# Transposes in two halves of 64 rows: probabilities and graph rows in a five-pass graph transformer

## The reference, cut to what matters

```python
x = _layernorm(x + _L0_gnn_ref(x, adj, adj, ...))   # 12-head attention, bias 2*adj, output product
x = _layernorm(x + _L1_gnn_ref(x, adj, ...))        # 12-head attention masked by adj > 0, no output product
x = _layernorm(x + _L2_gnn_ref(x, adj, ...))        # two graph layers, below
x = _layernorm(x + _L3_gnn_ref(x, adj, ...))        # 12-head attention, bias adj, output product

# one of the two graph layers
u = jnp.einsum('bid,bjd->bij', h, h) / temper
a = jax.nn.softmax(u, axis=-1)
delta = a * adjacency_matrix
attn = delta / (jnp.sum(delta, axis=-1, keepdims=True) + 1e-10)
hl, hs, hr = h @ wl.T + b_l, h @ ws.T + b_s, h @ wr.T + b_r
ctx = (attn * upper) @ hl + diag(attn)[..., None] * hs + (attn * lower) @ hr
h = jax.nn.relu(norm(ctx) * g + beta)
```

## Time and profile before

| | us |
|---|---|
| median of 3 executions | 2920.33 (2918.25 to 2920.56) |
| profiled execution, its own time | 2920.63 |
| its span, first to last instruction | 2918.9 |
| busy: PE matmul | 2676.6 (92%) |
| busy: PE weight load | 2351.3 (81%) |
| busy: DVE | 2204.6 (76%) |
| busy: ACT | 1441.8 (49%) |
| busy: POOL | 1906.2 (65%) |
| mean granted clock of PE | 0.963 |

### The profile page before, as it was taken

The page is one execution under the profiler, slowest core; times in us unless marked ns, Lnnn a source line. Parts: engine busy times, 40 slices in busy tenths (PEclk is TensorE's granted clock), DMA queues, the critical chain, the costliest instruction groups (busy, mean ns, idle before and its releaser), DMA issues. The chain is left out here.

```text
span 2918.9 us, 67000 instructions
## 1 busy us (share of the span) xinstructions
PE 2676.6 (92%) x22942; PEld 2351.3 (81%) x22942; DVE 2204.6 (76%) x3795; ACT 1441.8 (49%) x2968; POOL 1906.2 (65%) x2229
## 2 busy tenths in 40 slices
PE   7999999977999999599999888888887899999996
PEld 6888888866778778599999877777776688888885
DVE  4888888874777777577777667777777488888886
ACT  4555555535566666344444344444444455555553
POOL 2766766762666666577777567767776267766766
PEclk9999999988999999699999989999999999999998
DMA  3222222113222222312212132222221122222211
GB/s 108 70 67 68 66 66 68 55 42 96 78 76 81 81 76 63 99 53 68 64 55 67 56 102 71 69 68 71 69 68 48 57 70 67 68 66 68 66 58 39
DMA packets 179134, 200.54 MB, mean 69 GB/s; under 512 B 56516, under 2 KB 179016, under 8 KB 179016
## 3 DMA queue, kind: packets, MB, share of 16 engines
q1 hardware_dynamic: 179016, 198.99, 22.2%
HBM read 136.03 MB, written 62.91 MB: 68 GB/s over the span
## 5 line engine op out<-in xcount | busy, mean ns | idle before, releaser
L413 PE MATMUL l_ps_p<-l_xT,l_w 128*128 128x512 f32 x2592 | 677.5, 406 | 6.5 <-DVE l_xT L655 4.5
L1088 PE MATMUL l_ps_h<-l_w,l_hT 128*128 128x384 f32 x3456 | 678.9, 342 | 0.0
L1088 PEld LDWEIGHTS l_ps_h<-l_w,l_hT 128*128 128x128 f32 x3456 | 612.6, 191 | 2.6
L413 PEld LDWEIGHTS l_ps_p<-l_xT,l_w 128*128 128x128 f32 x2592 | 467.8, 189 | 110.7 <-issue 8.3
L342 POOL TENSOR_TENSOR l_pr<-l_sc,l_st 128x768 f32<-128x768 f32 x192 | 289.4, 1507 | 368.7 <-DVE l_st L693 341.1
L1178 ACT ACTIVATE l_hp<-l_hf 128x384 fp32r<-128x384 f32 x256 | 134.7, 526 | 474.5 <-DVE l_hf L1300 470.4
L312 POOL TENSOR_TENSOR v<-v,l_bvs 128x768 f32<-128x768 f32 x192 | 368.6, 1920 | 0.0
L999 POOL TENSOR_TENSOR l_hp<-l_hf,l_hp 128x384 fp32r<-128x384 f32 x256 | 272.0, 1062 | 134.4 <-ACT l_hp L1178 131.7
L407 PE MATMUL l_ps_p<-l_w,l_xT 128*128 128x384 f32 x1728 | 349.5, 347 | 7.6 <-ACT l_k L561 3.7
L574 ACT ACTIVATE v<-l_ps_p 64x192 f32<-64x192 f32 x768 | 250.5, 326 | 188.0 <-PE l_ps_p L407 179.1
L407 PEld LDWEIGHTS l_ps_p<-l_w,l_xT 128*128 128x128 f32 x1728 | 291.6, 188 | 27.3 <-issue 8.8
(11 more groups left out here) (129 smaller groups left out, 4761.1 us busy)
## 6 DMA issues: line engine op xcount, KB each, us to landing
rows<-l_yo SPq DMA_DIRECT2D x256, 192.0 KB, 1.9
l_xa<-rows SPq DMA_DIRECT2D x64, 768.0 KB, 5.0
l_xr<-rows SPq DMA_DIRECT2D x192, 192.0 KB, 2.4
l_xa<-in_x SPq DMA_DIRECT2D x16, 768.0 KB, 4.8
l_xr<-in_x SPq DMA_DIRECT2D x64, 192.0 KB, 2.4
out<-l_yo SPq DMA_DIRECT2D x64, 192.0 KB, 1.9
l_edge<-in_adj SPq DMA_DIRECT2D x80, 128.0 KB, 2.3
raw<-in_L_gnn_Wq SPq DMA_DIRECT2D x3, 576.0 KB, 5.8
```

The source lines that it names most:

```text
L413: last = nc.tensor.matmul(bank[:, :], W[m][:, l, t, o * P:(o + 1) * P], rows[:, r, t, :], start=c + t == 0, stop=c == 2 and t == KT - 1)
L1088: last = nc.tensor.matmul(ps_h[m][:, :D], hT[gpar][:, l, t, s * P:(s + 1) * P], W[m][:, r, t, :], start=c + t == 0, stop=m != SELF and c = ...
```

## The change

In `attention_pass`, `ps_t` becomes two tensors of one bank each, one for each graph of a unit. The six transposes of a unit become twelve: for each pair of heads one of the 64 rows of the first graph into the first bank, and one of the 64 rows of the second graph into the second. Both `pe_t` counts come at the last pair. ACT copies 384 elements from each bank. Before the transposes stands one wait for all older copies, and an instruction of its own that counts up a new semaphore, `pe_waited`, for which nobody waits.

In `digcn_pass`, the twelve transposes of a group become 24 in the same way, a bank for each graph. They are made in two steps: tiles 0 and 1 in unit 0 behind the left product, tile 2 in unit 1 behind the left product. ACT makes four copies for each step: 512 elements each in the first, 256 each in the second. The counts on `pe_x`, `act_x` and `act_f` are renumbered. This pass has a `pe_waited` too, counted up once ahead of each step. The transposes of rows in `attention_pass` (line 378), of attention (1073) and of weights stay whole.

```diff
+ROW_TILES = ((0, 1), (2,))
-        ps_t = a.ps("ps_t", [P, 2 * 512])
+        ps_t = [a.ps(f"ps_t{g}", [P, 512]) for g in range(GPU)]
...
@@ -440,13 +442,16 @@
                 if not inside(n, units):
                     return
                 pe.wait_ge(pool_p if wo else act_e, n + 1)
+                if counted(2 * n):
+                    pe.wait_ge(act_pT, 2 * n)
+                pe.sem_inc(pe_waited, 1)
                 for h in range(PAIRS):
-                    if h in (0, 4):
-                        if counted(2 * n - 1 + (h == 4)):
-                            pe.wait_ge(act_pT, 2 * n - 1 + (h == 4))
-                    last = nc.tensor.transpose(ps_t[:, h * P:(h + 1) * P], pr[b][:, 2 * h:2 * h + 2, :], ident[:, :])
-                    if h in (3, 5):
-                        last.then_inc(pe_t, 1)
+                    for g in range(GPU):
+                        q = slice(g * NODES, (g + 1) * NODES)
+                        last = nc.tensor.transpose(ps_t[g][:, h * NODES:(h + 1) * NODES], pr[b][q, 2 * h:2 * h + 2, :],
+                                                   ident[q, q])
+                        if h == PAIRS - 1:
+                            last.then_inc(pe_t, 1)
...
@@ -595,12 +600,12 @@
             def probs_T(n, b):
                 if not inside(n, units):
                     return
-                for half, (lo, hi) in enumerate(((0, 4), (4, 6))):
-                    act.wait_ge(pe_t, 2 * n + half + 1)
+                for g in range(GPU):
+                    act.wait_ge(pe_t, 2 * n + g + 1)
                     if counted(n - 1):
                         act.wait_ge(pe_o, n - 1)
-                    nc.scalar.activation(pT[b][:, lo:hi, :], ps_t[:, lo * P:hi * P].rearrange("p (h q) -> p h q", q=P),
-                                         ACT.Copy).then_inc(act_pT, 1)
+                    nc.scalar.activation(pT[b][:, :, g * NODES:(g + 1) * NODES],
+                                         ps_t[g][:, :D].rearrange("p (h q) -> p h q", q=NODES), ACT.Copy).then_inc(act_pT, 1)
...
-            sp.wait_ge(pe_x, KT)
+            sp.wait_ge(pe_x, 2)
...
-                        sp.wait_ge(pe_x, KT * (i + 2))
+                        sp.wait_ge(pe_x, 2 * (i + 2))
...
@@ -989,7 +995,7 @@
                 if not inside(g, groups):
                     return
                 for t in tiles:
-                    pool.wait_ge(act_x, KT * g + t + 1)
+                    pool.wait_ge(act_x, 4 * g + 2 + 2 * (t // 2))
...
-            def rows_T(g, gpar, tiles=range(KT)):
+            def rows_T(g, steps=range(2)):
                 if not inside(g, groups):
                     return
                 pe.wait_ge(s_xa, 16 * (g + 1))
-                for t in tiles:
-                    if counted(KT * g + t - 1):
-                        pe.wait_ge(act_x, KT * g + t - 1)
-                    for u in range(UNITS):
-                        last = nc.tensor.transpose(ps_x[(gpar + t) % 2][:, u * P:(u + 1) * P],
-                                                   xa[:, u, t * P:(t + 1) * P], ident[:, :])
+                for step in steps:
+                    if counted(4 * g + 2 * step):
+                        pe.wait_ge(act_x, 4 * g + 2 * step)
+                    pe.sem_inc(pe_waited, 1)
+                    for j, t in enumerate(ROW_TILES[step]):
+                        for u in range(UNITS):
+                            for b in range(GPU):
+                                q = slice(b * NODES, (b + 1) * NODES)
+                                c = (j * UNITS + u) * NODES
+                                last = nc.tensor.transpose(ps_x[b][:, c:c + NODES], xa[q, u, t * P:(t + 1) * P], ident[q, q])
                     last.then_inc(pe_x, 1)
 
...
-                pe.wait_ge(act_f, KT * (g + 1))
+                pe.wait_ge(act_f, 4 * (g + 1))
...
-                    pe.wait_ge(act_x, KT * (i + 1))
+                    pe.wait_ge(act_x, 4 * (i + 1))
...
-            rows_T(0, 0)
+            rows_T(0)
...
                     project(n, i, par, s, LEFT)
                     if s < 2:
-                        rows_T(i + 1, 1 - par, (2 * s,))
+                        rows_T(i + 1, (s,))
                     context(n - 1, ppar, ps)
                     project(n, i, par, s, RIGHT)
                     if s == 3:
                         attention_T(i + 1)
-                    if s == 0:
-                        rows_T(i + 1, 1 - par, (1,))
                     if s == 1:
                         products(i + 1, 1 - par)
                     project(n, i, par, s, SELF)
...
-            def rows_T(g, gpar, tiles=range(KT)):
+            def rows_T(g, gpar, steps=range(2)):
                 if not inside(g, groups):
                     return
-                for t in tiles:
-                    act.wait_ge(pe_x, KT * g + t + 1)
-                    bank = ps_x[(gpar + t) % 2]
-                    nc.scalar.activation(hF[gpar][:, t, :], bank[:, :], ACT.Copy).then_inc(act_f, 1)
-                    nc.scalar.activation(hT[gpar][:, 0, t, :], bank[:, :], ACT.Copy).then_inc(act_x, 1)
+                for step in steps:
+                    act.wait_ge(pe_x, 2 * g + step + 1)
+                    t, tiles = ROW_TILES[step][0], len(ROW_TILES[step])
+                    for b in range(GPU):
+                        bank = ps_x[b][:, :tiles * UNITS * NODES].rearrange("p (x q) -> p x q", q=NODES)
+                        for to, ready in ((hF[gpar][:, t:t + tiles, :], act_f), (hT[gpar][:, 0, t:t + tiles, :], act_x)):
+                            rows = to.rearrange("p t (u g q) -> p (t u) g q", g=GPU, q=NODES)[:, :, b, :]
+                            nc.scalar.activation(rows, bank, ACT.Copy).then_inc(ready, 1)
...
                     n, b = i * UNITS + s, s % 2
                     left_right(n, b, LEFT)
                     if s < 2:
-                        rows_T(i + 1, 1 - par, (2 * s,))
+                        rows_T(i + 1, 1 - par, (s,))
                     if s == 2:
                         attention(i + 1, 1 - par, 1)
                     normed(n - 2, pair * 4 + 2 * par + s // 2 - 1, b)
                     left_right(n, b, RIGHT)
-                    if s == 0:
-                        rows_T(i + 1, 1 - par, (1,))
                     standardise(n - 1, 1 - b)
```

More of the change, by code:

```diff
@@ L205, in attention_pass @@
         c_zero = a.sem("c_zero")
+        pe_waited = a.sem("pe_waited")
         pe_w, act_w, dve_w = a.sem("pe_w"), a.sem("act_w"), a.sem("dve_w")
```

## The result

The changed kernel takes 2930.08 us (median of 9 runs, 2927.82 to 2932.93). The kernel before, on the same chip, takes 2920.09. The ratio is 1.0033, 95% interval [1.0023, 1.0043]. The forecast was 2917.0 with a range from 2893 to 2940. The time lies in the range, but on the other side of no change. The profiled execution took 2932.93 us, with a span of 2931.0 us. It is the slowest of the nine, so the traces differ by 12.1 us where the medians differ by 10.0.

The account below looks back on a forecast made before the run. PE was taken to bound all but the second graph pass, where other engines set the pace. -6.3 + 1.7 + 1.2 = -3.4 us on 2920.63 us gave 2917, range 2893 to 2940.

Parts of the forecast that it names:

- In the second graph pass the 3.47 us cover it: Second graph pass: PE's 3.47 us wait for ACT's copies was said to hide the later rounding of the right product: 0.
- the third 256-element copy: Start of a graph pass: its end priced at 0.92 us, within 3.5 us from first copy to row products.
- Without cover it would be up to 16 x 0.62 = 10 us: Second graph pass: upper price of the later rounding if PE's wait did not hide it, up to 10 us.
- the rival of the counting instruction: PE's queue: the counting instruction after each wait holds the queue; +13 us, 2930 us, chance 0.18.
- Pace of the halves: Attention and graph passes: two half transposes run at once, 0.058 us a pair, against 0.109 for a whole one.
- That rival (0.109): Half transposes don't run side by side, 0.109 us a pair; +59 us, 2979 us, chance 0.08.
- Emptying: Weight block ahead of half transposes: the array empties at its end, 0.09 us.
- First load laid bare behind: Weight block behind half transposes: its first load is no longer hidden, 0.11 us.
- Three passes: The three attention passes, 48 groups at -0.132 us each: -6.3 us.
- the bound: Passes with an output product: most gain lost to transposes waiting for POOL's probabilities, 3 us; 0 was taken.
- First graph pass: First graph pass, PE always busy: seams outweigh the shorter stream by 0.11 us in 16 groups, +1.7 us.
- Starts: Starts of the two graph passes, where nothing hides the copies: 3.5 us instead of 2.94, together +1.2 us.

Follow-up runs that it names:

- e13: Changed kernel plus 24 matmuls of 256 columns, result never read, ahead of the products in the second graph pass: 2923.77 us.
- e5: Changed kernel with the counting instruction issued twice at each block of transposes instead of once: 2942.64 us.
- e7: Changed kernel, ACT's exact copies of both halves before the rounded ones, and unit 0's half 1 copies behind the rounding of the right product: 2919.54 us.
- e14: Kernel before, with POOL's three subtractions for the next group's rounded rows moved to the end of unit 2 in the second graph pass: 2901.71 us.
- e8: Changed kernel with ACT's exact copies of both halves ahead of both rounded ones in each graph-pass step: 2920.73 us.

## Why the prediction was wrong

**The failed step** is "In the second graph pass the 3.47 us cover it", with its 0. The 3.47 us are PE's wait for the copies. I had the rounding of the right product, and with it POOL, 0.62 us late, held that against PE's wait alone, and never asked whether the copies that end the wait come as early as before. They come 0.71 us later. One half was in my own numbers: I had the rounding end at 1425.9, so POOL begin later, but I followed only PE, who waits for that product, and not POOL's next instructions and what they do to DVE. The other half was in the same part too: at the start of the pass I priced the third 256-element copy, and in the steady groups I did not. The wait that I called a cover was the chain itself. (The two halves don't weigh the same: at full clock only DVE's is left, and the late copy costs through the clock alone, by e13.)

The clock is not in the prediction at all, though the earlier trace rows shows 0.95 there and 1.00 elsewhere; holding it up brought 10.8 us back (e13).

Two numbers of the prediction come near by chance. "Without cover it would be up to 16 x 0.62 = 10 us" is near the 11.9 measured, but it prices PE waiting for POOL's product. And the rival of the counting instruction stood at 2930, where the kernel landed, by +13 from that instruction; it took about 3, and the second graph pass the rest.

The other steps, by their own numbers:

- *Pace of the halves*, 0.058 us for a pair: a pair takes 0.062, the first 0.112, and a block and its seam take 0.52 us where I had 0.51. That rival (0.109) is out, and loads of 128 columns, two side by side, do not hold a pair at 0.107 us here.
- *Emptying*, 0.09: the weight block ahead of the transposes takes 0.095 more. Right.
- *First load laid bare behind*, 0.11: 0.02. Wrong in size. But the first load of a whole block, 0.06, was not on the path before either (0.63 from block to block, where I had 0.71), and so the difference holds: in the second pass units 0 and 1 gain 0.09 each (0.094), unit 2 loses 0.06 (0.056), unit 3 nothing (the wait took it, as said).
- *Three passes*, -6.3: they gave -0.2 a group in the second pass, against -0.13 (0.06 of it a shorter wait behind the values), and about -0.03 in the other two; with the first groups -1.5 us in all. There I handed back nothing to POOL, with 3 us as the bound. The counting instruction, which I took at 0 because the queue runs ahead, stands right behind that wait, where it can't run ahead: 0.10 a group. The rival was right in its mechanism on 64 of the 176 blocks I gave it, and wrong in the second pass, where a second one changed nothing (e5).
- *First graph pass*, +1.7: -0.3, or nothing. The two blocks take as long as the three did, and 0.095 is added ahead of each, but the seams around the third block, which is gone, give 0.19 back. I had today's three blocks at 1.31 us of stream, and from block to block they take 1.06.
- *Starts*, +1.2: +2.0. From the first copy to the products are 3.92 us in each pass, where I had 3.5.

Together these terms come to +0.2 where I had -3.4, so the change brings nothing even where the second graph pass loses nothing: e7, which has that pass back, took 2919.54 us, within the noise of before.

## What to carry to other kernels

An engine's idle time covers a delay only if what ends the idle time is not itself delayed: follow the changed order through the queue of each engine that it passes, to the copy that the wait names. In a stage where TensorE's granted clock is under 1.00, a late start is not worth its own length, but what the clock makes of it, and a shorter wait can pay more than it saves. VectorE operations with two inputs in SBUF and subtractions on GpSimd are worth moving apart; in this kernel that brought 18 us (e14).

## What the runs showed of the hardware that I had not expected

- The same 74 matmuls take 6.2, 7.5, 7.7 or 8.8 us, at granted clocks of 1.00, 0.80, 0.78 and 0.66, in a pattern that repeats every two or four groups. A start 0.27 us earlier changed the pattern, and with it 0.7 us a group (after and e8). At full clock a start 1.0 us later changed nothing (e8 and e13).
- Two VectorE operations on SBUF tensors beside GpSimd's subtractions took up to 1.6 us each instead of 0.56, and GpSimd's subtraction 1.60 instead of 1.26.
- A rolled loop's place in TensorE's program can cost 40 us: ten stalls of 2.3 to 3.2 us at five turns, 26.8 us together, and the lower clock behind them. 128 instructions ahead of it took them away.
- An instruction that only counts takes TensorE's queue 55 ns in a row of 128. Behind a wait that binds, the shortest time from GpSimd's end to the first transpose grew from 54 ns to 146 with one, and to 299 with two.
